# Attention whose outputs and row maxima are turned by VectorE, with output banks that change from head to head

## The reference

```
xn = layernorm(x)
Q, K, V = xn @ Wq.T + bq, xn @ Wk.T + bk, xn @ Wv.T + bv      # split into 16 heads
A = softmax(Q @ K.T / sqrt(16))
out = (0.6 * A + 0.4 * L) @ V                                  # L: a band of +-3 keys, rows sum to 1
x = x + out @ Wo.T + bo
xn = layernorm(x)
p = softmax(gelu(xn @ rW1 + rb1) @ rW2 + rb2);  top 2 of 4 experts per token
x = x + sum over the two experts of p_e * (gelu(xn @ We1[e] + be1[e]) @ We2[e] + be2[e])
```

## Time and profile before

| | us |
|---|---|
| median of 3 runs | 1991.43 (1991.3 to 1991.99) |
| span of the profiled execution | 2006.8 |
| PE (TensorE) busy | 1951.3, 97% of the span |
| DVE (VectorE) busy | 1626.5, 81% |
| ACT (ScalarE) busy | 1374.2, 68% |
| POOL (GpSimd) busy | 346.9, 17% |

### The profile page before, as it was taken

How to read it: one execution, slowest core, us unless ns; L and a number is a source line. 1 busy time by engine, 2 the same in 40 slices (tenths; PEclk the granted TensorE clock), 3 DMA queues, 4 the chain that set the end, 5 groups by cost and what they waited for, 6 DMA issues and landing times. The chain is left out here.

```text
span 2006.8 us, 47862 instructions
## 1 busy us (share of the span) xinstructions
PE 1951.3 (97%) x16384; PEld 1036.7 (52%) x16384; DVE 1626.5 (81%) x2075; ACT 1374.2 (68%) x2471; POOL 346.9 (17%) x379
## 2 busy tenths in 40 slices
PE   7999999999999999999999999999998799999997
PEld 3543333333333333333333333333687689999997
DVE  6799999999999999999999999994255565555564
ACT  3358888888888888888888888889544422233332
POOL 1361010001000100001000100010024532232233
PEclk9999999999999999999999999999999899999999
DMA  7954355335643454336534554341123677788884
GB/s 266 245 111 92 78 102 115 74 74 97 108 90 74 90 99 106 74 80 102 113 74 74 100 105 90 74 93 54 42 74 131 242 235 227 245 269 297 263 272 113
DMA packets 105849, 264.09 MB, mean 132 GB/s; under 512 B 20896, under 2 KB 52768, under 8 KB 99104
## 3 DMA queue, kind: packets, MB, share of 16 engines
q1 hardware_dynamic: 92624, 245.29, 48.6%
q0 software_dynamic: 13152, 17.83, 4.6%
HBM read 206.95 MB, written 73.94 MB: 140 GB/s over the span
## 5 line engine op out<-in xcount | busy, mean ns | idle before, releaser
L626 DVE TENSOR_REDUCE part_max<-psum 128x1 f32<-128x1024 f32 x1024 | 1240.8, 1222 | 50.6 <-PE psum L750 37.7
L681 ACT ACTIVATE probs<-psum 128x512 f32<-128x512 f32 x2048 | 1111.1, 596 | 145.4 <-PE psum L763 78.2
L763 PE MATMUL psum<-score_q,score_k 50*128 50x512 f32 x2048 | 745.9, 446 | 0.1
L750 PE MATMUL psum<-max_k,max_q 48*128 48x512 f32 x2048 | 737.9, 449 | 0.5 <-DVE part_max L626 0.4
L775 PE MATMUL psum<-probs,v_ones 128*32 128x256 f32 x8192 | 654.1, 391 | 9.4 <-ACT heads_sb L696 9.0
L763 PEld LDWEIGHTS psum<-score_q,score_k 50*128 50x128 f32 x2048 | 306.9, 184 | 404.7 <-ACT probs L681 390.7
L775 PEld LDWEIGHTS psum<-probs,v_ones 128*32 128x32 f32 x8192 | 162.1, 107 | 380.8 <-issue 198.1
L750 PEld LDWEIGHTS psum<-max_k,max_q 48*128 48x128 f32 x2048 | 294.2, 185 | 12.8 <-issue 7.0
L1184 ACT ACTIVATE x_sb<-psum,x_sb 128x512 f32<-128x512 f32 (+1 forms) x160 | 101.6, 636 | 257.8 <-PE psum L1564 243.1
L1583 PE MATMUL psum<-w,h_hi 128*128 128x256 f32 x1120 | 202.1, 279 | 2.7 <-DVE h_lo L1385 2.5
L1583 PEld LDWEIGHTS psum<-w,h_hi 128*128 128x128 f32 x1120 | 178.7, 189 | 13.8 <-DVE h_lo L1385 3.2
(11 more groups left out here) (185 smaller groups left out, 1352.3 us busy)
## 6 DMA issues: line engine op xcount, KB each, us to landing
w<-w_split SPq DMA_DIRECT2D x40, 2048.0 KB, 7.9
max_q<-qk_pieces SPq DMA_DIRECT2D x192, 128.0 KB, 7.2
score_k<-qk_pieces SPq DMA_DIRECT2D x192, 128.0 KB, 4.7
xs<-in_pads SPq DMA_DIRECT2D x33, 528.0 KB, 8.3
qk_pieces<-pieces SPq DMA_DIRECT2D x32, 512.0 KB, 4.6
w_split<-w_pair SPq DMA_DIRECT2D x32, 512.0 KB, 8.8
max_k<-qk_pieces SPq DMA_DIRECT2D x192, 64.0 KB, 8.2
score_q<-qk_pieces SPq DMA_DIRECT2D x192, 64.0 KB, 2.2
```

Source lines behind the costliest of these rows:

```text
L626: nc.vector.tensor_reduce(part_max[:, t, p:p + 1], ps_m[p].rearrange("q b f -> q (b f)"), axis=AXIS.X, op=ALU.max).then_inc(m_read, 1)
L681: nc.scalar.activation(probs[kb % 2][:, chunk * BLOCK:(chunk + 1) * BLOCK], bank_of(at), ACT.Exp, scale=float(HD) ** -0.5).then_inc(exp_do ...
L750: last = nc.tensor.matmul(ps_m[p][:, h, :], max_q[u][rows, t * P:(t + 1) * P], max_k[u][rows, p * BLOCK:(p + 1) * BLOCK], start=True, stop ...
L763: nc.tensor.matmul(bank_of(at), score_k[u][rows, kb * P:(kb + 1) * P], score_q[u][rows, part * BLOCK:(part + 1) * BLOCK], start=True, stop ...
```

## The change

The query columns of each block are stored in another order: column j, b, r of a head is token 128 b + 32 j + r of a block, so that 32x32 turns put an output where it belongs. TensorE reads its moving operand in that order at projection, and SP stores the queries in pieces of 128 columns (512 bytes) instead of 512 columns (2048 bytes).

The two turns leave TensorE and ScalarE. VectorE's `transpose` turns each 32x32 block of a tile by itself. `turn_heads` takes the 128x512 output bank from PSUM to `heads_tok` in one such instruction, behind the last maxima of a head; `turn_shift` makes `shift_row` in four instructions of 32x32, behind the maxima of kb = 12. `heads_sb`, its copy and the copies to `heads_tok` and `shift_row` are gone. The inversion moves from kb = 2 to kb = 0. The shift rows go out in two DMAs instead of four.

The output banks change: an even head uses bank 2, an odd one bank 3, and the bank that is not the output's belongs to the score ring. In kb = 1 chunk 2 takes the bank of the head before and waits for its turn (`heads_turned`), and chunk 1 waits for the exponential two before it instead of three.

The diff, cut to its core:

```diff
@@ project, SP @@
-                            dst = dram["qk_pieces"][qk, head:head + HEADS // KD, :, :, ds((n % BPS) * BLOCK, BLOCK)]
-                            sp.dma_start(dst.rearrange("h d c t -> (h d) c t"),
-                                         pieces[u][:, qk, m, :, :].bitcast(F32)).then_inc(stored[u], 16)
+                            rows = dram["qk_pieces"][qk, head:head + HEADS // KD, :, :, :]
+                            rows = rows.rearrange("h d c t -> (h d) c t")
+                            src = pieces[u][:, qk, m, :, :].bitcast(F32)
+                            if qk == 0:
+                                dst = rows.rearrange("p c (j n) -> p c j n", j=BPS)[:, :, :, ds((n % BPS) * P, P)]
+                                src = src.rearrange("p c (j n) -> p c j n", j=BPS)
+                            else:
+                                dst = rows[:, :, ds((n % BPS) * BLOCK, BLOCK)]
+                            sp.dma_start(dst, src).then_inc(stored[u], 16)
@@ project, PE @@
-                            done = nc.tensor.matmul(ps_qk[j], w["qk"[qk]][:, k, m * P:(m + 1) * P],
-                                                    xnT[:, ds(n, 1), k, :].squeeze(1),
+                            rows = xnT[:, ds(n, 1), k, :].squeeze(1)
+                            if qk == 0:
+                                rows = rows.rearrange("p (b j r) -> p j b r", b=BT, j=BPS)
+                            done = nc.tensor.matmul(ps_qk[j], w["qk"[qk]][:, k, m * P:(m + 1) * P], rows,
@@ attend @@
+    FIRST_RING, RING_OF, OUT_OF = ((0, 1, 2), (1, 0, 3)), ((1, 0, 3), (0, 1, 2)), (2, 3)
+    def s_done(n, kb, c):
+        return n * UNITS + CH * kb + c + 1
+    def score_bank(u, kb, c):
+        at = CH * kb + c
+        return psum[:, FIRST_RING[u][at % RING] if at < CH else RING_OF[u][(at - CH) % RING], :]
+    def out_bank(u):
+        return psum[:, OUT_OF[u], :]
-    SHIFT_DMAS = PIECES * ROW_TILES
+    SHIFT_DMAS = ROW_TILES
@@ attend, SP @@
             for h in range(ROW_TILES):
-                for c in range(PIECES):
-                    row, first = h * ROW_TILE + STACK + c, c * ST + h * ST // ROW_TILES
-                    sp.dma_start(score_q[u][row:row + 1, :].bitcast(F32).rearrange("o (t q) -> o t q", q=P),
-                                 shift_row[first:first + ST // ROW_TILES, :].bitcast(F32)).then_inc(shift_in[u], 16)
+                row = h * ROW_TILE + STACK
+                sp.dma_start(score_q[u][row:row + PIECES, :].bitcast(F32).rearrange("c (t q) -> c t q", q=P),
+                             shift_row[h * n:(h + 1) * n, :]).then_inc(shift_in[u], 16)
...
-                    sp.wait_ge(exp_done, count_of(shift_unit(n)))
+                    sp.wait_ge(shift_turned, n + 2)
@@ attend, DVE @@
+        def turn_shift(m):
+            dve.wait_ge(shift_ready, m + 1)
+            rows = shift[:].rearrange("p h c t -> p (h c t)").bitcast(F32)
+            for q in range(0, P, QUAD):
+                last = nc.vector.transpose(shift_row[:, q:q + QUAD], rows[q:q + QUAD, :])
+            last.then_inc(shift_turned, 1)
+
+        def turn_heads(n, u):
+            dve.wait_ge(pv_done, ST * (n + 1) + PV_OPEN)
+            dve.wait_ge(tok_used, n + 1)
+            nc.vector.transpose(heads_tok[:].rearrange("p t e -> p (t e)"), out_bank(u)).then_inc(heads_turned, 1)
...
-                    if kb == HEADS_AT + 1:
+                    if kb == INVERT_AT:
                         invert(n)
                     if ahead == ST - 1 and not (last and u):
                         split_shift(n + 1)
+                    if kb == SHIFT_AT and not (last and u):
+                        dve.wait_ge(shift_in[u], 16 * SHIFT_DMAS * (i + 1))
+                        turn_shift(n + 1)
+                turn_heads(n, u)
@@ attend, ACT @@
-                    if kb == ST - 1:
-                        copy_o(n)
-                    if kb == HEADS_AT:
-                        copy_tok(n)
-                    if kb == SHIFT_AT and not ends:
-                        act.wait_ge(shift_in[u], 16 * SHIFT_DMAS * (i + 1))
-                        copy_shift(shift_unit(n))
@@ attend, PE @@
+        def scores(n, kb, u, c):
+            if kb == 1 and c == RING - 1:
+                pe.wait_ge(heads_turned, n + 1)
+            else:
+                held = 2 if kb == 1 and c == 1 else RING
+                if not isinstance(n, int) or s_done(n, kb, c) > held:
+                    pe.wait_ge(exp_done, s_done(n, kb, c) - held)
...
-                if kb == 0:
-                    pe.wait_ge(o_copied, n + 1)
...
-                    if kb == HEADS_AT:
-                        wait_bank(heads_unit(n))
-                        pe.wait_ge(o_copied, n + 1)
-                        transpose_heads(bank_of(heads_unit(n))).then_inc(s_ready, 1)
-                    if kb == SHIFT_AT and not ends:
-                        wait_bank(shift_unit(n))
-                        wait_apart(pe, count, shift_ready, n + 2, ones_set, POOL_SET)
-                        transpose_shift(bank_of(shift_unit(n))[0:PIECES * ST, 0:P]).then_inc(s_ready, 1)
```

More of the change, by code:

```diff
@@ L408, in attend @@
     RING = 3
[L409 to L427, removed]
-    SHIFT_DMAS = PIECES * ROW_TILES
+    UNITS = CH * ST
+    INVERT_AT = 0
+    FIRST_RING, RING_OF, OUT_OF = ((0, 1, 2), (1, 0, 3)), ((1, 0, 3), (0, 1, 2)), (2, 3)
[7 more added lines that the diff above has]
+    SHIFT_DMAS = ROW_TILES
     PARTS = 2
@@ L458, in attend @@
     BANKS = VB * BLOCKS
-    SHIFT_HALF = 2 * (ST + 1)
     FIRST_SCORES = 2 * LOOK - CH
@@ L469, in v_tiles_before @@
         return spread if half < FIRST_SCORES else min(TILES, TILES - 2 + half - FIRST_SCORES)
-    BANKS_BEFORE_SHIFT = v_tiles_before(SHIFT_HALF) // 2
-    ps_v = [ps_s[r % VB] for r in range(BANKS - 1)] + [ps_o]
+    ps_v = [psum[:, r % VB, :] for r in range(BANKS - 1)] + [psum[:, OUT_OF[1], :]]
     def v_tiles(b, vb):
@@ L674, in _, with exp @@
         act.sem_inc(pv_done, PV_OPEN)
-        def exp(n, kb, c, ends):
-            at, chunk = unit(n, kb, c, ends), CHUNKS[c]
+        def exp(n, u, kb, c):
+            chunk = CHUNKS[c]
             if c == 0:
                 act.wait_ge(pv_done, ST * n + kb - 1 + PV_OPEN)
-            act.wait_ge(s_ready, count_of(at))
-            nc.scalar.activation(probs[kb % 2][:, chunk * BLOCK:(chunk + 1) * BLOCK], bank_of(at), ACT.Exp,
+            act.wait_ge(s_ready, s_done(n, kb, c))
+            nc.scalar.activation(probs[kb % 2][:, chunk * BLOCK:(chunk + 1) * BLOCK], score_bank(u, kb, c), ACT.Exp,
                                  scale=float(HD) ** -0.5).then_inc(exp_done, 1)
[L684 to L696, removed]
         def copy_v(b, vb, bank):
@@ L701, in copy_v @@
                                  ).then_inc(v_copied, 1)
-        with act.Fori(0, BANKS_BEFORE_SHIFT // VB) as b:
+        with act.Fori(0, BANKS // VB - 1) as b:
             for vb in range(VB):
-                copy_v(b, vb, ps_s[vb])
-        for r in range(BANKS_BEFORE_SHIFT // VB * VB, BANKS - 1):
-            if r == BANKS_BEFORE_SHIFT:
-                act.wait_ge(first_tr, 1)
-                nc.scalar.activation(shift_row[:], ps_shift, ACT.Copy).then_inc(first_copied, 1)
-            copy_v(r // VB, r % VB, ps_v[r])
+                copy_v(b, vb, ps_v[vb])
+        copy_v(BANKS // VB - 1, 0, ps_v[0])
         for c in range(CH):
-            exp(0, 0, c, False)
+            exp(0, 0, 0, c)
             if c == 1:
-                copy_v((BANKS - 1) // VB, (BANKS - 1) % VB, ps_o)
+                copy_v(BANKS // VB - 1, 1, ps_v[BANKS - 1])
         def body(i, last):
@@ L752, in maxima, with values @@
             last.then_inc(m_ready, 1)
-        def wait_bank(at):
-            if not isinstance(at[0], int) or at[0] + at[1] >= RING:
-                pe.wait_ge(exp_done, at[0] + at[1] - RING + 1)
-        def scores(n, kb, u, c, ends):
-            at = unit(n, kb, c, ends)
-            wait_bank(at)
+        def scores(n, kb, u, c):
[5 more added lines that the diff above has]
+                    pe.wait_ge(exp_done, s_done(n, kb, c) - held)
             h, part = CHUNKS[c] // ROW_TILES, CHUNKS[c] % ROW_TILES
             rows = slice(h * ROW_TILE, h * ROW_TILE + SROWS)
-            nc.tensor.matmul(bank_of(at), score_k[u][rows, kb * P:(kb + 1) * P],
+            nc.tensor.matmul(score_bank(u, kb, c), score_k[u][rows, kb * P:(kb + 1) * P],
                              score_q[u][rows, part * BLOCK:(part + 1) * BLOCK], start=True, stop=True
                              ).then_inc(s_ready, 1)
-        def values(n, kb, u, part, ends):
+        def values(n, kb, u, part):
             if part == 0:
-                pe.wait_ge(exp_done, count_of(unit(n, kb, CH - 1, ends)))
-                if kb == 0:
-                    pe.wait_ge(o_copied, n + 1)
+                pe.wait_ge(exp_done, s_done(n, kb, CH - 1))
             at = part * BLOCK // PARTS
             for j in range(BPS):
```

(31 more changed lines are left out.)

67 lines of the change are left out of this document (23 added, 44 removed).

## The result

| | median us of 4 runs | lowest to highest | span of the profiled execution |
|---|---|---|---|
| before | 1991.45 | 1991.3 to 1991.99 | 2006.8 |
| after | 1970.64 | 1970.48 to 1970.84 | 1969.0 |

The change makes the kernel 20.8 us faster, about 1%: a ratio of 0.9896 with a 95% interval of 0.9882 to 0.991. The forecast was 28 us, 1963.5 us, with a range of 1955 to 1984. Sign and place were right, and 7 us of the expected gain are missing.

A forecast was written before the change was run, and what follows sets the result against it. TensorE's own instructions were taken to bound attention. Terms -35.8 + 6.8 + 1 = -28 us, taken from the median of 1991.43, gave 1963.5 us (1959 to 1968 with the turn at 0.6 to 0.8 us); range 1955 to 1984.

The forecast's parts named there:

- The bound: Attention: TensorE's own instructions set the pace, a half step (two score matmuls, half a key block's values) taking 1.24 us.
- The removed part, 35.8 us: Taken off TensorE in attention: 31 shift turns 6.2 us, 33 output turns 19.1, 31 waits between heads 10.5.
- The small turns at key block 12, 1 us: VectorE's four 32x32 shift turns ahead of key block 13's maxima: 0.3 to 0.65 us long, 1 us in all.
- the cover: At key block 12, VectorE delay hidden before a bank pair is rewritten: 0.49 us, less 0.05 for the release.
- The seam, 6.8 us: Between two heads, key block 1's chunk 2 score waits for VectorE's output turn: 0.22 us, 31 times.
- the first delay: Between two heads, key block 1's chunk 1 score waits for key block 0's last exponential: some 0.1 us late.
- Rival B: Between heads: output turn as quick as the conversion, 0.45 us, only the late exponential left; about 1958 us; chance 0.09.
- The front, 0 to 1 us: Before attention: query stores in 512 byte pieces make ScalarE's copies end later; taken as 0, up to 1 us.
- Rival E: Before attention: a query packet costs 87 ns whatever its size, maxima start some 35 us later; 1998 us; chance 0.07.
- Rival D: In attention VectorE pays whole durations, no overlap: 41.0 us a head against 40.79; about 1998 us; chance 0.05.
- rival A: Between heads: output turn takes two cycles a column, 1.22 us, costing 23 us in all; about 1981 us; chance 0.15.

The follow-up runs named there:

- four turns more: Changed kernel with four added 32x32 turns behind the four of the shift, all reading partitions 0 to 31 into a spare tile: 1983.58 us.
- the half turn: Changed kernel, where VectorE turns only the first 256 columns of a head's outputs: 1970.49 us.
- the second profile: The kernel before, unchanged, profiled once more: 1990.93 us.
- the short exponential: Changed kernel, where the last exponential of key block 0 of each head makes only 256 of its 512 columns: 1965.13 us.
- the one-turn version: Changed kernel with the shift turned by one 128x32 instruction between key block 11's two reductions, and eight DMAs of 128 byte pieces: 1959.12 us.

## Why the prediction was right or wrong

**The bound: right.** TensorE's own instructions set the pace, and taking instructions and waits from between them took time away nearly one for one.

**The removed part, 35.8 us: right.** The three gaps are gone in every head. Added up over the trace of before, from attention's first values to its last, they were 18.4 us at the output turns (32 of them), 6.4 at the shift turns and 11.0 at the seams, 35.7 together; the output turn behind the last head lies outside that.

**The small turns at key block 12, 1 us: this is the term that was mis-sized.** They cost 7.1, 0.22 to 0.29 in each of 30 heads. The step that failed is the price of one turn. The bounds of 0.075 and 0.16 a start came from small operations that all start at the same partition; these turns move on by a quarter each time, and then they don't overlap at all: 0.21 from start to start. The pause was 0.76 us, above the upper bound of 0.65, and "at 0.65 it costs 0.2" was right as a mechanism: a pause beyond the cover is paid in every head. The cover, worked out as 0.44, is about 0.5: 0.76 less the gap here, and 1.26 less the gaps of 0.70 to 0.78 with four turns more. The text had 6.5 us as the end of this term and took 1, without a row for turns that move on by a quarter. The sentence "no gap at key block 12" was the one to be looked for, and it fell. The Trainium skill has the rule, in "VectorE: DVE Perf Modes", section "Two Vector instructions with no wait between them": an instruction whose input starts in another quadrant (a group of 32 partitions) than the last read of that memory starts only when every earlier one has finished. The 0.21 against the 0.10 agree with it. I cited that page for its DRAIN and for bf16 turns, and passed over the section that bore on this.

**The seam, 6.8 us: the size was right, the working only half.** Measured 0.18 to 0.20 a head (0.24 at the last seam), 6.0 us. The turn's length, 0.69 from the nearest row, is 0.705. (The estimate from the Trainium skill, "VectorE: DVE Perf Modes", section "The three transpose paths", was 0.71, and the trace agrees.) But the text let the turn decide alone and contain the first delay of 0.1. In fact the late exponential alone costs 0.2: its score starts 0.1 late, at 610.94 instead of 609.93 + 0.57 + 0.34 = 610.84, and then takes 0.50, where such a score in a half step without a delay takes 0.39. The values are 0.2 late, and by then the turn, ended at 611.18 + 0.705 = 611.89, no longer delays the score of 611.94, which is 0.57 behind the values. The turn's own price was worked out well: with the exponential out of the way it holds chunk 2 back by 0.19, and the text had 0.16 to 0.26. Where the text failed is the first delay, taken as 0.1 and contained in the second, where it costs 0.19 by itself. Rival B, a quick turn, would therefore have won nothing here: the half turn, at 0.440, did not.

**The front, 0 to 1 us: the cause was elsewhere.** Attention's first values come 1.1 us later; of that 0.9 are a wait that the text did not count (from the first maxima to the first values it is 51.9 and 51.8 us in the two traces of before, 52.7 in after). In front of the first head the small reduction, a cast, a subtraction and the turns stand on VectorE one after the other. VectorE's and TensorE's rows in the kernel after:

```profile
117.86 0.19 DVE L626 TENSOR_REDUCE neg_max<-part_max 128x16 f32<-128x32 f32 x1
...
118.57 0.84 DVE L634 STREAM_TRANSPOSE shift_row<-shift 32x32 f32<-32x32 f32 x4
119.35 4.56 DVE L618 TENSOR_REDUCE part_max<-psum 128x1 f32<-128x1024 f32 x4
```

```profile
120.57 0.51 PE L725 MATMUL psum<-max_k,max_q 48*128 48x512 f32 x2 [1.12 <-DVE part_max L618]
```

The reductions pause for 119.35 - 117.86 = 1.49 us there, and the maxima wait 1.12, where in the kernel before they wait 0.18 behind the small reduction.

**Rival E, the query stores: refuted.** The DMA queue and SP's stores of the second sequence in the kernel after, 57.8 to 79.3 us:

```profile
q1 hardware_dynamic: 9250, 7.27, 109.1%
```

```profile
58.29 21.03 SPq L239 DMA_DIRECT2D qk_pieces<-pieces  x16
```

9250 packets where 4058 were the earlier trace rows, 1.091 x 16 x 21.5 / 9250 = 0.041 us each on the mean of small and large pieces, where the large ones took 0.087. The packets of 512 bytes alone took 0.028 in that stretch of the trace, less than the 0.036 that was taken. The stores take 21.03 us, before 21.27. TensorE reads the strided queries at the old rate, 3.60 us a block, as in the earlier trace rows.

**Rival D, whole durations on VectorE: refuted** for reductions, which run on at (6.89 - 1.214) / 5 = 1.135 us from start to start, at 1.214 each. For the small turns whose source moves on it is what happened.

**The sum.** 35.7 off, 6.0 for the seam, 7.1 for the small turns leave 22.6; attention lost 22.9 between its first values and its last, the front gave back 1.1 and the untouched rest 1.2 (564.7 against the second profile's 563.5; over the traces of the experiments on the kernel after it lies between 563.2 and 564.9). That leaves 20.6, beside 20.8 of the medians. Against the forecast the small turns make 6.1 of the 7.1 us that are missing. The wide range holds the measured time because it takes in rival A, whose mechanism did not happen: the forecast's own 1959 to 1968, for a turn of 0.6 to 0.8 us, does not, though the turn took 0.705. Two readings of before were poor: the 15.4 us by which the profile lay over the median were put down as a constant, and were mostly one execution's; and the period of 40.79 was one of two that alternate, mean 40.70. Neither changed the sum, which was made from gaps.

## What to carry to other kernels

Where a step moves to an engine that looks free, count how long that engine is away from the work that paces the kernel, and compare it with the cover at that very place: here 0.34 us were hidden, and of 0.76 us what went beyond some 0.5 came out in every head. Price several small instructions by rows that change what these change, here the partition at which the source starts, and see whether one larger instruction does the same: the 128x32 turn costs what one 32x32 turn costs. When two new waits end within a tenth of a microsecond of each other, undo both before judging either.

## What the runs showed of the hardware

- VectorE's transpose of fp32 took 705 ns for 128x512 from PSUM, 440 ns for 128x256, 202 ns for 128x32 and 198 ns for 32x32 with a source that moves from quarter to quarter (167 with one that stays).
- Small turns whose source moves to another quarter of the partitions start 0.21 us apart, those whose source stays some 0.10.
- A half step of the same instructions lies, in all these traces, near one of three lengths: 1.227 us, 1.231 and 1.236 in turn, or 1.240. It keeps one of them over many half steps and changes it only within a few half steps of a place where something else cuts in (the seam, the small reduction of `neg_max`, the turns, the inversion). Which one follows differs from kernel to kernel; with the short exponential and with the one-turn version this was worth 3.2 to 3.5 us of attention. Nothing that was run here tells why.
